# Graph network kernel: the seven loads of a dense block's tables become four

## The reference, cut to what matters

```python
h = jnp.maximum(_layernorm(x, axis=-1), 0.0)
agg = jax.ops.segment_sum(h_nb[edge_src], edge_dst, num_segments=n)      # L0, twice
out = jax.ops.segment_sum(messages, dst, num_segments=num_nodes)         # L1
out = jax.ops.segment_sum(msg, dst, num_segments=num_nodes)              # L2, three times
...
e = jnp.concatenate([h[src], h[dst]], axis=-1)                           # L3, for each edge
e = jax.nn.relu(e @ Wm1 + bm1) @ Wm2 + bm2
m = jax.ops.segment_sum(e * drop_mask, dst, num_segments=n)
```

## Time and profile before

| what | value |
|---|---|
| runs | 9792.88, 9795.44, 9819.64 us; median 9795.44 us |
| the profiled execution | 9824.99 us, of which the span from first to last instruction is 9823.0 us |
| first pass | to about 1636 us |
| passes 1 to 5 | about 1636 to 7463 us |
| edge network and the last nodes | from there to 9823 us |
| loads of table pieces | 1925 = 5 passes x 55 blocks x 7, 224 KB each |
| mean granted TensorE clock | 0.898 of full speed |

### The profile page before, as it was taken

One profiled execution on the slowest core, in us unless ns is written; L12 is line 12 of the kernel. 1 busy time (PEld: TensorE's weight loads), 2 busy tenths in 40 slices (PEclk: granted clock), 3 DMA queues, 4 the chain that ended last, 5 costly groups with the idle time before them and its releaser, 6 DMA issues. The chain is left out here.

```text
span 9823.0 us, 153063 instructions
## 1 busy us (share of the span) xinstructions
PE 7816.8 (80%) x53210; PEld 5849.9 (60%) x53210; DVE 3559.2 (36%) x7241; ACT 1548.1 (16%) x3109; POOL 5604.4 (57%) x5798
## 2 busy tenths in 40 slices
PE   2898887888878888788887888788886777777777
PEld 1666665566556666565665656566665666666666
DVE  6777774233322222222221222222223333333333
ACT  3666663000000000000000000000000111111111
POOL 2555554555546665555546655555554666666665
PEclk9999998999989999899998989899987888888888
DMA  5232223444445555544454444545544444444443
GB/s 104 91 101 94 98 95 124 135 138 138 140 145 145 147 147 145 152 136 136 138 162 124 138 132 137 153 137 144 142 140 116 122 121 125 120 123 124 121 124 110
DMA packets 756942, 1268.18 MB, mean 129 GB/s; under 512 B 286469, under 2 KB 584648, under 8 KB 749592
## 3 DMA queue, kind: packets, MB, share of 16 engines
q1 hardware_dynamic: 476340, 779.09, 25.4%
q0 software_dynamic: 185344, 371.98, 16.2%
q10 hardware_dynamic: 94948, 113.19, 3.4%
HBM read 1076.55 MB, written 194.22 MB: 129 GB/s over the span
## 5 line engine op out<-in xcount | busy, mean ns | idle before, releaser
L2293 PE MATMUL PS<-PARTS,work 128*128 128x288 bf16 x26950 | 3898.9, 300 | 631.2 <-issue 626.3
L2293 PEld LDWEIGHTS PS<-PARTS,work 128*128 128x128 fp8e4 x26950 | 2731.6, 102 | 1627.8 <-issue 878.3
L736 POOL DMA_INDIRECT GF<-table,SRC x2262 | 2257.6, 998 | 1561.5 <-issue 614.9
L747 POOL DMA_INDIRECT GF<-newparts,SRC x1760 | 1674.1, 951 | 1447.6 <-PE PS L2275 658.3
L747 POOL DMA_INDIRECT work<-newparts,SRC x1735 | 1643.5, 947 | 1093.6 <-PE PS L2275 534.5
L2239 PE MATMUL PS<-work 128*96 128x128 f32 x3126 | 597.5, 371 | 490.9 <-issue 259.7
L2412 PE MATMUL PS<-PARTS,work 128*128 128x289 bf16 x5390 | 981.4, 293 | 0.0
L1078 ACT ACTIVATE work<-PS 128x396 fp8e4<-128x396 f32 x1760 | 825.7, 501 | 552.2 <-PE PS L2349 435.1
L2239 PEld LDWEIGHTS PS<-work 128*96 128x96 f32 x3126 | 546.4, 237 | 521.7 <-issue 521.2
L2349 PE MATMUL PS<-FREE 128*128 128x396 bf16 x1760 | 600.9, 343 | 238.9 <-ACT work L1078 123.8
L1719 DVE TENSOR_TENSOR work<-PS,REL 128x1024 bf16<-128x1024 f32 (+1 forms) x636 | 771.3, 1213 | 0.4 <-issue 0.4
(11 more groups left out here) (276 smaller groups left out, 5848.2 us busy)
## 6 DMA issues: line engine op xcount, KB each, us to landing
work<-amat SPq DMA_DIRECT2D x1925, 224.0 KB
work<-in_dst_dram SPq DMA_DIRECT2D x195, 512.0 KB
amat<-work SPq DMA_DIRECT2D x55, 1568.0 KB
work<-in_edge_attr_dram SPq DMA_DIRECT2D x195, 384.0 KB
GF<-table,SRC POOLq DMA_INDIRECT x2262
PARTS<-newparts SPq DMA_DIRECT2D x35, 1008.0 KB, 7.1
GF<-newparts,SRC POOLq DMA_INDIRECT x1760
work<-newparts,SRC POOLq DMA_INDIRECT x1735
```

Source lines behind the costliest of these rows:

```text
L736: pool.indirect_dma_start(G[:, k, i, 0:D], None, table_rows[a % 2], bass.IndirectOffsetOnAxis(ap=SRC[:, tile:tile + 1], axis=0)).then_inc( ...
L747: pool.indirect_dma_start(GP[g % PLACE][:, i, :], None, part_rows[a % 2], bass.IndirectOffsetOnAxis(ap=SRC[:, tile:tile + 1], axis=0)).the ...
L2293: last = pe.matmul(PS[:, DENSE_B[b], 0:PQ], AB[m][:, jj * WIN:(jj + 1) * WIN].bitcast(FP8), PARTS[:, j * PQ:j * PQ + PQ], start=(j == 0), ...
```

## The change

The seven loads of a block become four: pieces 0 and 1 in one transfer, 2 and 3, 4 and 5, and piece 6 alone. A pair's load waits until PE has finished the second piece of the pair. PE waits for a load only at m = 0, 2, 4 and 6; the nop stays ahead of every piece. Semaphores `d_ld` are left for those four. The same bytes move: rows of 3584 bytes a partition for a pair. In `new_parts` the order becomes P0 P1 A01 P2 A23 P4 P5 A45 A6.

```diff
+LOADS = ((0, 2), (2, 2), (4, 2), (6, 1))
+LOADED = [m for m, n in LOADS]
...
+        AB_BYTES = work[:, 2048:2048 + AC * ACW // 4].bitcast(U8)
...
-        d_ld = [sem(f"d_ld{m}") for m in range(AC)]
+        d_ld = {m: sem(f"d_ld{m}") for m in LOADED}
...
-            def load_piece(d, b0, m):
-                sp.wait_ge(d_mm, d * AC + (b0 * AC + m + 1))
+            def load_pieces(d, b0, m, n):
+                sp.wait_ge(d_mm, d * AC + (b0 * AC + m + n))
                 sp.nop(nofuse=True)
-                sp.dma_start(AB[m], amat_rows[bass.ds(d * P, P), m * ACW:(m + 1) * ACW]).then_inc(d_ld[m], 16)
+                sp.dma_start(AB_BYTES[:, m * ACW:(m + n) * ACW], amat_rows[bass.ds(d * P, P), m * ACW:(m + n) * ACW]
+                             ).then_inc(d_ld[m], 16)
 
             def load_block(d, b0):
-                for m in range(AC):
-                    load_piece(d, b0, m)
+                for m, n in LOADS:
+                    load_pieces(d, b0, m, n)
...
                         if m not in (3, 6):
                             load_parts(a, (m,))
-                        load_piece(0, a * DB, m)
+                        for first, n in LOADS:
+                            if m == first + n - 1:
+                                load_pieces(0, a * DB, first, n)
...
                 def piece(d, b, m):
-                    pe.wait_ge(d_ld[m], d * 16 + (b0 - DB + 1) * 16)
+                    if m in LOADED:
+                        pe.wait_ge(d_ld[m], d * 16 + (b0 - DB + 1) * 16)
```

## The result

The change makes the kernel 2.2% faster: a ratio of 0.9777 (95% interval 0.9758 to 0.9797), 218 us of 9794 (199 to 237). Its median is 9555.3 us (9548.1 to 9569.2), outside the forecast range of 9720 to 9855. (The two medians, 9794.16 and 9555.3, are 239 us apart; the ratio is not taken from the medians alone.

A forecast was written before the change was run, and what follows sets the result against it. The prediction took a loop of PE and POOL, with PE's unexplained stops in it and the loads outside, to bound passes 1 to 5. Its terms summed to 0 on the median of 9795.44: forecast 9795 us, range 9720 to 9855.

The forecast's parts named there:

- SP issues less: SP's queue in passes 1 to 5: 275 us of issuing go, all within SP's 3532 us of waiting; value 0.
- the loads are not part of that loop: Claim that PE and POOL alone close a slot in a loop, with table loads off the path.
- a gain of at most those 275 us: Other end of the term on SP's issues, if SP's waiting did not cover the saved queue time.
- PE's nops: PE's queue: 825 nops lose their wait but still execute at 51 ns; value 0, other end -42 us.
- A pair comes later: Load of an even piece starts one piece later, landing with 1.4 us to spare; value 0, other end +60 us.
- pairs arrive late: Rival: at the tight spot pairs land too late for PE, 9855 us, or 9916 at twice a turn; chance 0.14.
- Between the passes: Start of a pass, A0 now behind P1: pair lands just in time; value 0, other end +1 us.
- the 10.3 that I had set as a mark: Sign against the forecast: pass 1 starting more than 10.3 us after its first load at 1625.67.
- Larger rows: DMA queues: POOL's small rows wait behind larger ones, 484 us if each group were waited for; value 0.
- The sum: All terms added to the median: 0 + 0 + 0 + 0 = 0, ends -42 and +61, forecast 9795 us.
- The first rival: PE's stops shrink with the 15% fewer transfers: 149 us gained, 9646 us, or 9721 at half; chance 0.20.
- the crawl: Few microseconds around a slot's end when PE gets instructions one or a few at a time; 985.5 us of stops.

The follow-up runs named there:

- v1: Kernel before with SP's wait ahead of each load given five times, on a chip with long stops: ratio 1.0216, +211 us.
- c2_seven_waits: Changed kernel, but PE waits at all seven pieces again, against the kernel before on a chip with long stops: 0.9828, -173 us.
- x4: Changed kernel with 64 bytes of padding behind each piece in DRAM, rows of 1792 bytes, on a chip with short stops: 7969.4 us, 1.0007 against the kernel before.
- w1: Kernel before with each piece's load as four rows of 448 bytes a partition, on a chip with long stops: ratio 1.0020.
- w2: Kernel before with an already met wait and a nop ahead of every second matmul of a piece, on a chip with long stops: 1.0480, +483 us.
- z1: Kernel before with every second gather of passes 1 to 5 left out: 0.8269 on a chip with long stops, 4.5% faster with short ones.

## Why the prediction was wrong

**The step that failed** is "SP issues less ... Value 0". Its working looked at whom SP's queue makes wait, found nobody, and was right in that: SP waits 4100 us after. But SP's instructions cost PE time although nobody waits for them: `v1`, which adds waits on SP alone, is 211 us slower. What the prediction had wrong ahead of it is "the loads are not part of that loop". The term measures -173 us (-141 to -205, `c2_seven_waits`), and even its other end, "a gain of at most those 275 us", held only by accident, as it was SP's time and not PE's.

**PE's nops.** "The nop stays for all seven pieces" is true of the code and wrong of the trace: 810 of them are not there (the prediction counted 825, but 15 carry the wait for PARTS). The term measured -18 us alone, with an interval that holds 0, and -41 as the difference of 214 and 173, near its end of -42 where 0 was taken.

**A pair comes later**: 0, as predicted. PE waits for no table load in the changed kernel. Late loads begin at two a block (56 us) and at four a piece (279 us), so the rival "pairs arrive late" was rightly given little.

**Between the passes**: PE's first piece came 11.7 us after the first load, beyond the 10.3 that I had set as a mark. PE was itself busy with the nodes' layers until 1598.25 and then stopped for 1.02 us, "issue"; one microsecond, once, at most.

**Larger rows**: 0 as far as is known. By the Trainium skill, DMA: Bandwidth & Descriptors, section on queues, rings and completion order, the prediction let gathers wait longer behind larger rows, 484 us if each did. Nothing here speaks for it: larger rows (`x4` against the change) make no difference where POOL sets the pace, and smaller ones (`w1`) gained nothing where the stops are long; the larger rows themselves were not tried alone on such a chip. The fixed cost of 2.0 us that the prediction took from the same page of the Trainium skill stands there in a section on transfers that POOL issues, and these loads are SP's; no run here times it.

**The sum** by the price of `w2`, which shares nothing with the change but the chips' kind, would have been 4890 x 0.042 = 205 us, against 218 (199 to 237). That is partly luck: `w2` prices nops of PE, five sixths of the 4890 are SP's, and SP's waits measured 0.027.

**The first rival** had the direction and the place, and was given 0.20. It scaled the crawl by transfers, 15% of 985.5 = 149 us; the stops shrank by 24%, or about 21% without the waits for PARTS, and the clock gave another 101 us of busy time that the rival didn't have. What spoke against it, that the worst crawl stood where SP had issued nothing for 27 us, was read too strongly: it shows that the loads aren't needed for a crawl, and not that they don't add to it. `z1` shows what is needed, the gathers: with half of them the stops are nearly gone.

What is shown: the long stops come with POOL's gathers, and not in every measurement of the same kernel; where they are, fewer instructions of SP make the passes shorter and more of SP or PE make them longer, by 0.027 to 0.045 us each; some two fifths of that is busy time of PE at a lower clock, the rest idle time. What is not shown is what the gathers and the instructions share there, why that runs short on some chips only, and whether an issue of DMA costs more than another instruction. One rival, the loading of the instructions themselves, was not tried; the packets of the DMA queues of kind "instruction" hardly moved (168 and 142 before, 167 and 140 after, 180 and 141 in `w2`), which speaks against it. The Trainium skill, NOTIFIC — the notification-queue block, section 7.1, Overflow: three behaviours, one of which stalls the engine, says that the block which writes out the records of instructions holds engines back when its internal pipeline fills; a price for each recorded instruction, whatever its engine, and none for a nop that isn't recorded would fit that, if the lower price of SP's waits is left aside. No run here shows it: none was made without records, and the unrecorded nop may as well not exist.

## What to carry to other kernels

When PE stands in mid-stream for nothing that the profile shows, count the instructions of all engines, also of those that are idle most of the time, and price an edit by that count beside its waits and transfers; a transfer that is cut in seven has more address work too. Look at PE's busy time for the same matmuls as well as at its stops: here the granted clock moved with them and made some two fifths of the effect. Find the price with an amplified edit (thousands of waits that are met already) before arguing over small ones. And measure on more than one chip: here the same edit is worth 2.2% on some and nothing on others, whose passes POOL bounds.

## What the runs showed of the hardware that was not expected

- The same kernel takes 7960 us on some chips and 9766 to 10069 on others. Not only the passes differ (4532 and 5587 us, both of the changed kernel): its first pass takes 1423 and 1599 us, its edge network 2017 and 2361.
- On the slower kind, PE's matmuls restart in steps of 0.70 us, mostly one to three at a time, around the end of a group of eight gathers; with four gathers a group the stops are 85 us in place of about 1000.
- PE's busy time for the same 33,350 matmuls of the passes was 4097 us at a mean granted clock of 0.98, 4627 at 0.92, 4728 at 0.91, 5037 at 0.87 and 5159 at 0.85.
- Nops without a wait left no instruction in the trace: 810 of 1925.
- Four times as many rows in SP's DMA queue, 448 bytes in place of 1792, cost 20 us of 10057 (0 to 40).
